# Dispatch of a soft mixture of experts: logits made one batch ahead, two batches of logits on chip, two sets of PSUM banks used in turn

## The reference, cut to what matters

```python
logits = einsum('bnd,esd->bnes', x, se)            # 4 batches, 2048 tokens, 16 experts x 64 slots = 1024 columns
dispatch = softmax(logits, axis=1)                 # over the tokens of a batch
combine = softmax(logits.reshape(b, n, -1), -1)    # over the 1024 slots of a token
slots = einsum('bnd,bnes->besd', x, dispatch)      # weighted sums of tokens: 1024 slots x 256 for each batch
```

## Time and profile before

| | us |
|---|---|
| median of three runs (2926.79 to 2930.8) | 2928.39 |
| profiled execution, its own time | 2925.22 |
| span of its trace | 2923.5 |
| stage `dispatch` within it: first load of `yT` to the first load of `experts` | 1885.70 to 2417.06 |
| TensorE busy over the whole span | 2644.7 (90%) |

### The profile page before, as it was taken

The page is one execution under the profiler, slowest core; times in us unless marked ns, Lnnn a source line. Parts: engine busy times, 40 slices in busy tenths (PEclk is TensorE's granted clock), DMA queues, the critical chain, the costliest instruction groups (busy, mean ns, idle before and its releaser), DMA issues. The chain is left out here.

```text
span 2923.5 us, 48961 instructions
## 1 busy us (share of the span) xinstructions
PE 2644.7 (90%) x16291; PEld 1583.8 (54%) x16291; DVE 2060.6 (70%) x5020; ACT 1609.4 (55%) x3282; POOL 440.4 (15%) x586
## 2 busy tenths in 40 slices
PE   4867999999999999999999999879797888979999
PEld 2434444444444444444444444357586677879999
DVE  6868898999999999999999999153442511226665
ACT  1540776777777777777777777653444531112221
POOL 1223011111111101111111111213224030030000
PEclk9985999999999999999999999989898988989999
DMA  3995343233033203321330000132232407755664
GB/s 121 317 293 61 44 57 42 29 43 43 11 39 43 36 13 45 43 27 22 43 43 8 8 7 7 41 153 94 94 133 75 151 7 241 221 170 190 191 198 149
DMA packets 191593, 259.52 MB, mean 89 GB/s; under 512 B 66820, under 2 KB 138632, under 8 KB 189864
## 3 DMA queue, kind: packets, MB, share of 16 engines
q1 hardware_dynamic: 170632, 237.17, 32.7%
q10 hardware_dynamic: 20768, 19.93, 2.1%
HBM read 155.16 MB, written 100.70 MB: 88 GB/s over the span
## 5 line engine op out<-in xcount | busy, mean ns | idle before, releaser
L665 ACT ACTIVATE att_pr<-att_ring 128x512 f32<-128x512 f32 (+3 forms) x2560 | 1173.4, 549 | 459.4 <-PE att_ring L742 452.3
L692 DVE TENSOR_REDUCE att_mx<-att_ring 128x1 f32<-128x512 f32 x1536 | 960.4, 682 | 81.4 <-PE att_ring L755 79.4
L755 PE MATMUL att_ring<-att_ks,att_qs 48*128 48x512 f32 (+3 forms) x2560 | 887.2, 439 | 59.6 <-DMA att_v<-v_rows 34.0
L742 PE MATMUL att_ring<-att_qs,att_ks 64*128 64x512 f32 (+3 forms) x2560 | 781.5, 409 | 15.4 <-DMA att_qs<-att_mrow 10.8
L742 PEld LDWEIGHTS att_ring<-att_qs,att_ks 64*128 64x128 f32 x2560 | 414.1, 187 | 557.2 <-DVE att_mx L692 250.9
L781 PE MATMUL att_acc<-att_pr,att_v 128*32 128x512 f32 (+3 forms) x5120 | 605.6, 545 | 2.2 <-ACT att_cT L672 1.5
L755 PEld LDWEIGHTS att_ring<-att_ks,att_qs 48*128 48x128 f32 x2560 | 418.5, 190 | 251.3 <-ACT att_pr L665 143.8
L698 DVE CUSTOM_DVE_ANT_0 att_junk<-att_ring,w_causal 128x512 bf16<-128x512 f32 (+3 forms) x1024 | 465.9, 487 | 64.7 <-PE att_ring L755 45.6
L642 POOL TENSOR_SCALAR_AFFINE_SELECT att_pr<-att_pr 128x512 f32<-128x512 f32 x256 | 162.4, 634 | 1191.9 <-ACT att_pr L665 1191.9
L1201 ACT CAST com_e1h<-com_tp 128x1024 fp32r<-128x1024 f32 x64 | 64.5, 1014 | 263.1 <-PE com_tp L1274 236.9
L998 PE MATMUL dis_lp<-dis_y,dis_lg 128*128 128x257 f32 x512 | 120.6, 400 | 83.0 <-ACT dis_lg L885 83.0
(11 more groups left out here) (140 smaller groups left out, 3016.4 us busy)
## 6 DMA issues: line engine op xcount, KB each, us to landing
slot_exps<-dis_e SPq DMA_DIRECT2D x64, 512.0 KB, 2.6
com_e<-slot_exps SPq DMA_DIRECT2D x64, 512.0 KB, 3.5
att_qs<-q_parts SPq DMA_DIRECT2D x96, 256.0 KB, 10.0
q_parts<-proj_part SPq DMA_DIRECT2D x32, 512.0 KB, 4.0
att_ks<-k_parts SPq DMA_DIRECT2D x96, 128.0 KB, 10.6
y_rows<-proj_y SPq DMA_DIRECT2D x16, 512.0 KB, 4.5
y_cols<-proj_yT SPq DMA_DIRECT2D x16, 512.0 KB, 5.1
context<-att_cn SPq DMA_DIRECT2D x64, 128.0 KB, 2.1
```

Of the source, the lines that this page charges most:

```text
L665: nc.scalar.activation(pr[:, s % NPR, h, off:CH], ring[:, bank_of["s", s, h], off:CH], ACT.Exp, scale=float(HD) ** -0.5).then_inc(exp_done, 1)
L692: nc.vector.tensor_reduce(dst, ring[:, bank, :], AX.X, ALU.max).then_inc(mb_used, 1)
L742: nc.tensor.matmul(ring[:, bank_of[e], off:CH], ks[r, g, kb * P:(kb + 1) * P], qs[r, g, c, hf * CH + off:(hf + 1) * CH], start=True, stop= ...
L755: nc.tensor.matmul(ring[:, bank_of[e], 0:wd], qs[r, g, c, q0:q0 + P], ks[r, g, j * CH:j * CH + wd], start=True, stop=True).then_inc(mb_rea ...
```

## The change

`dispatch` is written out over a list of phases, and no longer as a hardware loop. With L(b) for the logits of batch b and P(b, h) for the slot product of its half h, every engine walks through L(0), L(1), P(0,0), P(0,1), L(2), P(1,0), P(1,1), L(3), P(2,0), P(2,1), P(3,0), P(3,1).

- `lg`, `nr`, `zr` and `cm` hold two batches. Phase i uses the set `ps[:, i % 2]` of four PSUM banks.
- A half is divided, turned and stored during the phase after it (`turn` after tile 3 of a logits phase or before tile 6 of a product phase).
- The first six subtractions and exponentials of batch b-1 (`AHEAD`) are placed in the last six tiles of L(b), one per tile. The other 26 are in the product phases. All subtractions are VectorE's.
- The column maximum is reduced in place in `cm`, both halves in succession.
- `yT` is loaded straight into `yTl` and split in place, in a ring of three chunks. The first chunk is split by VectorE, the others by GpSimd.
- `y` is a ring of two chunks of four tiles. Each product phase reads the batch's four chunks again, so there are 32 loads of `y` instead of 16. Chunk m is loaded when chunk m-2 has been used.
- Three tensors of the earlier stages are released before `dispatch`, to make room.

```diff
+    RING = 3
+    AHEAD = 6
+    PHASES = [("L", 0), ("L", 1)]
+    for b in range(B):
+        PHASES += [("P", b, 0), ("P", b, 1)] + ([("L", b + 2)] if b + 2 < B else [])
-        y = a.sb("y", [P, TPB, D + 2])
-        lg = a.sb("lg", [P, TPB, NS])
+        y = a.sb("y", [P, 2, TPC, D + 2])
+        lg = a.sb("lg", [P, 2, TPB, NS])
-        lp = a.ps("lp", [P, 4, 512])
-        dp = a.ps("dp", [P, 4, 512])
+        ps = a.ps("ps", [P, 2, 4, 512])
...
 # SyncE
+                def load_y(m):
+                    if m < NYC:
+                        if m >= 2:
+                            sp.wait_ge(d_free, TPC * (m - 1))
...
+                    if ph[0] == "L":
+                        b = ph[1]
+                        for t in range(TPB):
+                            sp.wait_ge(e1_ready, b * TPB + t + 1)
+                            sp.dma_start(scr["e1"][b, t], e1[:, t % 2]).then_inc(e_out[t % 2], 16)
+                            if t % TPC == TPC - 1:
+                                load_yT(b * CPB + t // TPC + RING)
+                            if turned and t == 7:
+                                slots_out(turned)
+                        sp.dma_start(scr["zr"][b], zr[:, b % 2, :]).then_inc(z_out[b % 2], 16)
+                    else:
+                        for c in range(CPB):
+                            load_y(half_of(ph) * CPB + c + 2)
+                            if turned and c == 1:
+                                slots_out(turned)
...
 # ScalarE
+                        for t in range(TPB):
+                            act.wait_ge(lp_ready, b * TPB + t + 1)
+                            nc.scalar.copy(lg[:, b % 2, t, :], ps[:, i % 2, 2 * (t % 2):2 * (t % 2) + 2, :]
+                                           .rearrange("p a n -> p (a n)")).then_inc(lg_ready, 1)
+                            if t > 0:
+                                token_exp(b, t - 1)
+                            if b >= 1 and t >= TPB - AHEAD:
+                                exp_tile(b - 1, t - (TPB - AHEAD))
+                            if turned and t == 5:
+                                keep_slots(i - 1, turned)
+                        token_exp(b, TPB - 1)
...
 # VectorE, at the end of each tile t of a logits phase
+                            if b >= 1 and t >= TPB - AHEAD:
+                                less_max(b - 1, t - (TPB - AHEAD))
...
 # GpSimd
+                for b in range(B):
+                    if b:
+                        column_maxes(b - 1)
+                    for n in range(b * CPB, b * CPB + CPB):
+                        split(n + RING)
+                column_maxes(B - 1)
...
 # TensorE, in a logits phase
+                            if t >= 2:
+                                pe.wait_ge(lg_ready, b * TPB + t - 1)
...
+                            if turned and t == 3:
+                                turn(i - 1, turned)
```

More of the change, by code:

```diff
@@ L788, in dispatch @@
     HB = SB // 2
+    RING = 3
[3 more added lines that the diff above has]
+        PHASES += [("P", b, 0), ("P", b, 1)] + ([("L", b + 2)] if b + 2 < B else [])
+    half_of = lambda ph: 2 * ph[1] + ph[2]
+    early = lambda b: range(AHEAD) if b + 1 < B else range(0)
     with ExitStack() as ctx:
@@ L841, in batch @@
[L841 to L862, removed]
+                def load_yT(n):
+                    if n < B * CPB:
+                        if n >= RING:
+                            sp.wait_ge(lp_ready, TPC * (n - RING + 1))
+                        sp.dma_start(yTl[:, n % RING].bitcast(F32),
+                                     scr["yT_in"][n // CPB, n % CPB]).then_inc(yT_in[n % RING], 16)
@@ L894, in _ @@
                                                  scale=w["gbT"][:, k:k + 1],
                                                  bias=w["gbT"][:, DK + k:DK + k + 1]).then_inc(slT_kept, 1)
+                for i, ph in enumerate(PHASES):
+                    turned = PHASES[i - 1] if i and PHASES[i - 1][0] == "P" else None
+                    if ph[0] == "L":
+                        b = ph[1]
+                        if b >= 2:
+                            act.wait_ge(d_free, 2 * TPB * (b - 1))
+                        for t in range(TPB):
[9 more added lines that the diff above has]
+                        token_exp(b, TPB - 1)
+                    else:
+                        _, b, hf = ph
+                        for t in range(TPB):
+                            if hf or t not in early(b):
+                                exp_tile(b, hf * TPB + t)
+                            if turned and t == 9:
+                                keep_slots(i - 1, turned)
@@ L920, in _ @@
[L920 to L936 removed]
+                    nc.vector.tensor_tensor(lg[:, b % 2, t, h], lg[:, b % 2, t, h], cm[:, b % 2, h],
+                                            ALU.subtract).then_inc(sub_done, 1)
@@ new lines, in slots @@
+                def slots(i, ph):
+                    x = half_of(ph)
+                    dve.wait_ge(d_free, TPB * (x + 1))
+                    for q in range(HB):
+                        s = ph[2] * HB + q
+                        nc.vector.reciprocal(rz[:, s:s + 1], ps[:, i % 2, q, D:D + 1]).then_inc(rz_ready, 1)
+                    for q in range(HB):
+                        s = ph[2] * HB + q
+                        dve.wait_ge(rz_ready, x * HB + q + 1)
+                        if x:
+                            dve.wait_ge(slT_ready, (x - 1) * HB + q + 1)
+                        nc.vector.tensor_scalar(sl[:, q, :], ps[:, i % 2, q, 0:D], rz[:, s:s + 1], None,
+                                                ALU.mult).then_inc(sl_ready, 1)
@@ new lines, in released, with turn @@
+                def released(i):
+                    if i >= 2:
+                        ph = PHASES[i - 2]
+                        if ph[0] == "L":
+                            pe.wait_ge(lg_ready, TPB * (ph[1] + 1))
+                        else:
+                            pe.wait_ge(slT_kept, DK * HB * (half_of(ph) + 1))
+                def turn(i, ph):
+                    x = half_of(ph)
+                    for q in range(HB):
+                        pe.wait_ge(sl_ready, x * HB + q + 1)
+                        for k in range(DK):
+                            last = nc.tensor.transpose(ps[:, i % 2, q, k * P:(k + 1) * P], sl[:, q, k * P:(k + 1) * P],
+                                                       w["ident"][:])
+                        last.then_inc(slT_ready, 1)
```

296 lines of the change are left out of this document (149 added, 147 removed).

## The result

The changed kernel takes 2850.65 us (median of four runs, 2847.03 to 2859.1) against 2927.59 us for the kernel before in the same comparison (2924.78 to 2930.8). The ratio is 0.974, with a 95% interval of 0.972 to 0.977: 76.9 us faster. Forecast was 2859 us.

The account below looks back on a forecast made before the run. TensorE bounds the stage, with a 20 us hole per batch. From first logits matmul to last product, 411.6 us of work plus waits gave 448.3 instead of 516.5; with 1.1 at the start, 2859 us, range 2843 to 2875 (0.60).

Parts of the forecast that it names:

- pure work: TensorE's work without waits, first logits to last product: logits 179.2, cold start 2.3, product 224.0, turns 6.1; sum 411.6 us.
- chain in the last tiles of L(1) to L(3): Last six tiles: copy, maxima, subtraction, exponential wait in turn, 4.74 us per tile; 4.0 us per phase, 12.0 in all.
- tile 5: First product half after L(1) to L(3): TensorE waits 1.6 us for tile 5's exponential; 4.8 us in all.
- loads of `y`, tile 8: Product half after L(1) to L(3): load delayed in SP's queue, TensorE waits 3.3 us each; 9.9 in all.
- VectorE beside GpSimd: L(1) to L(3): two collisions of GpSimd's splits with VectorE's column maxima per chain; 1 us per phase, 3.0 in all.
- falls of the clock: Pauses of TensorE drop its clock to the half level, one fall per batch at 2 us; 6.0 us in all.
- the rival without waits: ScalarE's and VectorE's lag is absorbed and the clock does not fall: 2823 us; chance 0.13.
- the rival of several falls per batch: Clock falls in the chain, at tile 5 and at tile 8 for each of three batches: 2871 us; chance 0.10.
- the one that ends slower than before: Clock stays at half level through product phases, a half taking 56 us instead of 28: 2943 us; chance 0.02.
- It can only be filled by work of another batch: TensorE's 20 us hole per batch between logits and product: no engine near its limit, only another batch fills it.
- GpSimd's queue in L(1): Split of L(1)'s last chunk done at about 32.5 us against 33.6 when TensorE wants it: hidden by 1 us.
- Start and end: First split takes 2.3 us on VectorE instead of 3.4 on GpSimd, 1.1 us gained; what comes behind the stage keeps its form.

Follow-up runs that it names:

- e7: The changed kernel with ScalarE's early exponential of each tile made one tile later, VectorE's order kept; 2825.05 us.
- e4: The changed kernel with VectorE's early subtraction put ahead of the tile's maxima in the last six tiles of a logits phase; 2827.91 us.
- e5: The changed kernel with three chunks of `y` on chip instead of two; 2847.29 us.
- e8: e3 with GpSimd's fourth split of L(1) and L(2) put behind that batch's column maxima; 2850.47 us.
- e9: e3 with the last two of GpSimd's four splits of L(1) and L(2) put behind that batch's column maxima; 2846.48 us.
- e2: The kernel before with all subtractions on VectorE and both column maxima in succession on GpSimd; 2904.83 us.
- e3: The changed kernel with `AHEAD = 0` instead of 6, so no early subtractions or exponentials; 2844.72 us.

## Why the prediction held, point by point

The forecast was 448.3 us for the stretch; it is 439.8. By its terms, with what the profile of the changed kernel shows:

| term | forecast, us | measured, us | from |
|---|---|---|---|
| pure work | 411.6 | 411.5 | e7: 414.1 less 2.6 of waits |
| chain in the last tiles of L(1) to L(3) | 12.0 | 10.8 | 3 x 3.6, at 4.55 us per tile |
| tile 5 | 4.8 | 3.1 | 3 x 1.02, the wait in P(2,0) |
| copies of the turned half | 1.0 | 0.9 | 0.44 + 0.43 |
| loads of `y`, tile 8 | 9.9 | 5.6 | 2.49 + 1.90 + 1.25 |
| VectorE beside GpSimd | 3.0 | 5.9 | 1.42 + 2.53 + 0.31 in the chain, 2 x 0.84 at tile 5 |
| falls of the clock | 6.0 | 1.7 | the one in P(0,0); another was hidden |
| sum | 448.3 | 439.5 | 439.8 in all |

From copy 10 to the start of the product it took 19.01, 20.12 and 17.91 us. Less the excess over 4.55 us between two copies (1.42, 2.53, 0.31), each is 17.6, against 14.0 for five tiles without a wait: 3.6. The terms are good to about 1 us each. They leave out that TensorE loses 0.26 us more than its idle time at a wait (a tile behind one takes 3.06 us, 1988.69 to 1991.75, instead of 2.80), and that e7 lost 0.4 us more than the changed kernel at its start.

So the waits came where the forecast put them and for its reasons. That the sum is within 9 us has some luck in it: one term was half of what it should have been, and five others were too large.

- **The closed chain** was right in place, cause and size. The forecast was 4.74 us per tile, the copies are 4.55 apart. Two of the estimate's steps are shorter, column maximum to subtraction (1.13 instead of 1.22) and exponential to copy (0.53 instead of 0.61). e4 and e7 show the cause by two different cuts, and their 2828 and 2825 us are about what the rival without waits had (2823).
- **Pure work**: 128 records at 0.217 us are 27.8 us and not 28.0, 1.8 us less in eight halves. The measured figure holds the 0.26 us for each of e7's five waits and its longer start, which make up for it.
- **Tile 8's load**: right in mechanism, too large by 4.3 us. I gave 3.3 us to all three. TensorE reached tile 8 2.7 us behind the load's issue in each (2.4 in the forecast). From issue until TensorE went on it was 5.24, 4.65 and 3.91 us, and I had 5.7 throughout. In L(3), the last, no `yT` load stands ahead.
- **The clock**: two falls instead of three, and one of them cost nothing. Behind the wait of 2.49 us in P(0,0) the granted clock fell to 0.50, the 1.2 GHz level. It also fell in the chain of L(2), behind the wait of 2.57 us that ended at 2099.72:

```profile
2016.00:2018.00 2.00, 2.00 (x6) 1.54 (x6) 0.95 (x2) 1.61 (x3) 1.92 (x2) 0.50 0.11 33
2018.00:2020.00 2.00, 2.00 (x8) 1.64 (x7) 0.00 (x0) 0.00 (x0) 2.00 (x1) 0.71 0.00 0
...
2102.00:2104.00 2.00, 2.00 (x5) 1.09 (x4) 0.66 (x2) 1.31 (x2) 0.00 (x0) 0.50 0.46 186
```

The 112 records from 2014.79 took 26.23 us, where 0.217 us each and the last one's end are 24.5. In L(2) the tile took 1.3 us longer than one at the full clock, but the next could not start before its copy: TensorE waited 0.18 us for it instead of 1.49, and the tiles stayed 4.55 us apart. In e5 the wait at the same place is 2.58 us and the clock stayed at 1.00, with the tiles as far apart. It stayed at 1.00 in the chains of L(1) and L(3) too, with 1.5 us of idle time in each 4.55, and behind the waits of 1.90 and 1.25 us. So the rival of several falls per batch, and the one that ends slower than before, did not come. Before the change, the half level behind the first hole lasted 5.5 us and not 4 (0.50 from 1959.89 to 1965, 0.90 over the next 2 us); its cost of 2.6 us was read rightly.
- **VectorE beside GpSimd**: here I misread a row of before. The maximum that took 0.43 us more started at 1902.77, when the split that had begun at 1900.59 had only 0.55 us left of its 2.73. I took the loss for the price of any collision and set it against the rule that the one that comes second is blocked for the other's whole instruction, which it fits. In e8 the maximum starts 0.07 us behind the split and takes 3.37 us, which is its own 1.21 and 2.16 of the split's 2.35. That is the rule of the Trainium skill (SBUF — State Buffer, "SBUF: two separate sides"): of a VectorE operation with two inputs in SBUF and a GpSimd operation that reads SBUF, the one that starts first has the shared ports for its whole instruction. The traces agree, less 0.12 to 0.14 us: what was left of the GpSimd operation was 0.55, 2.28, 2.33 and 2.29 us (before, e8, L(2) of the changed kernel, e5), and VectorE lost 0.43, 2.16, 2.19 and 2.16. e9 shows that TensorE pays for it. In the changed kernel it cost 5.9 us, twice my 3.0 and less than the 14 that a full block of 2.34 at each of six collisions would be; not all of them fell at a split's start or where VectorE was late.
- **"It can only be filled by work of another batch"** was wrong. e2 takes 6.5 us of the 20.15 away and fills nothing. The sum did not suffer, since it started from pure work and not from parts of the change; a forecast for a part of the change would have.
- **GpSimd's queue in L(1)** was estimated to be 1 us ahead of TensorE; it was just behind, by 0.17 us (1980.05). The second reduction cost little, 3.84 us for both.
- **Start and end**: TensorE's wait ahead of the first logits fell from 10.83 to 8.56 us, 2.3 us where I had 1.1. The part behind the last product was 3.6 us longer, where the forecast kept it. In e2, with the order of before, it was 518.6 us, so this much is scatter between executions. `attend` was 9 us longer in this profile and 5 us shorter in e3's (it ended at 1878 there); what sets either is open.

## What to carry to other kernels

A piece of work that is put between two others on in-order engines can close a loop: ScalarE's next copy waited for an exponential, that for a subtraction, and that for the maxima of the copy before. Look for such loops by writing down one round of waits over all engines, and open them at one point: issue the result one tile later (e7) or its input ahead of the new wait (e4). Price each edit of a larger change separately: here a third of the gain could be had by taking GpSimd off the path alone, and six early subtractions cost 3.7 us in the closed loop and gave 22.0 once it was open. And before a collision is priced from one row, look how much of the other instruction was left when it began.

The best version is e7 (e4 is equal within its scatter): 2825.05 us, 3.5% faster than the kernel before, with 414.1 us in a stretch whose pure work is 411.5 us.

## What the runs showed of the hardware

- A tensor operation with two inputs on VectorE, started 0.07 us behind one on GpSimd (e8), took 3.37 us instead of 1.21. In the changed kernel a smaller one took 2.87 us beside a split and 1.52 beside a cast (1981.00) instead of 0.68. Each time VectorE lost what was left of the GpSimd operation, less 0.12 to 0.14 us.
- GpSimd took 6.95 us from a column reduction to its next subtraction. In e2 a cast follows the reductions at once, and the 6.93 us stand between the cast and the next split. Two reductions in succession took 3.59 us there, with no such gap between them.
- The granted clock stayed at full level in L(1) and L(3) with TensorE idle a third of the time in pauses of 1.5 us. It fell behind waits of 2.49 and 2.57 us, and not behind one of 2.58 us in e5.
